# Two transformer layers on one core: a new order of the blocks in each Mamba pair

## The reference

```python
proj = hidden_states @ in_proj_w                 # gate 4096, x 4096, B 128, C 128, dt 64
hbc = silu(causal_conv4(hbc) + conv_b)           # x, B and C
dt = softplus(dt + dt_bias); cum = cumsum(dt * A)            # within a chunk
scores = (C_c @ B_c) * exp(cum_i - cum_j) * dt_c             # i >= j
Y_diag = scores @ x_c
states = (exp(cum_last - cum) * dt_c, B_c, x_c)              # then scanned over the chunks
Y_off  = (C_c, prev_states) * exp(cum)
hidden = (Y_diag + Y_off + D * x) * silu(gate)
hidden = hidden * rsqrt(mean(hidden**2) + EPS) * norm_w
out = hidden @ out_proj_w
```

## Time and profile before

| | |
|---|---|
| runs | 1966.39, 1969.08, 1969.34 us; median 1969.08 |
| profiled execution | 1966.99 us, of which the span 1965.2 |
| TensorE busy | 1911.9 us, 97% of the span |
| VectorE, ScalarE, GpSimd busy | 1532.6, 1310.2, 830.7 us |
| granted TensorE clock, mean | 0.994 |

### The profile page before, as it was taken

The page is one execution under the profiler, slowest core; times in us unless marked ns, Lnnn a source line. Parts: engine busy times, 40 slices in busy tenths (PEclk is TensorE's granted clock), DMA queues, the critical chain, the costliest instruction groups (busy, mean ns, idle before and its releaser), DMA issues.

```text
span 1965.2 us, 43300 instructions
## 1 busy us (share of the span) xinstructions
PE 1911.9 (97%) x12642; PEld 1607.5 (82%) x12642; DVE 1532.6 (78%) x2860; ACT 1310.2 (67%) x2983; POOL 830.7 (42%) x997
## 2 busy tenths in 40 slices
PE   7999999999999999999999999999999999999998
PEld 7888778888888968888878886888888888788886
DVE  6886678888788468888878836888888883688886
ACT  4663389999555148888845514888875551588885
POOL 2210268888200016777710001777770000177776
PEclk9999999999999999999999999999999999999999
DMA  6330356656422114444422211544442221244442
GB/s 231 120 120 1 124 162 207 203 193 208 134 75 85 52 46 156 146 155 148 164 77 84 75 62 35 168 146 157 146 153 86 91 62 49 83 146 156 146 153 78
DMA packets 122051, 239.86 MB, mean 122 GB/s; under 512 B 10832, under 2 KB 48912, under 8 KB 121872
## 3 DMA queue, kind: packets, MB, share of 16 engines
q1 hardware_dynamic: 122000, 239.18, 37.2%
HBM read 198.37 MB, written 37.62 MB: 120 GB/s over the span
## 4 chain that ended last, share of the span: by engine, by line
PE 71%; issue 20%; DVE 5%; ACT 2%; POOL 1%; DMA 0%; POOLq 0%; DVEq 0%; ACTq 0%
PE bank L695 31%; PE bank L965 12%; PE bank L952 6%; PE bank L941 5%; PE bank L932 4%; PE bank L924 3%; PE both L695 2%; PE bank L845 2%; PE bank L802 2%; DVE conv_acc L1428 1%; PE both L802 1%; PE bank L772 1%; PE bank L777 1%; PE bank L854 0%; ACT bank L1166 0%
## 5 line engine op out<-in xcount | busy, mean ns | idle before, releaser
L695 PE MATMUL bank<-xn_r,w_r 128*128 128x512 f32 x2268 | 610.6, 409 | 4.2 <-issue 3.2
L695 PEld LDWEIGHTS bank<-xn_r,w_r 128*128 128x128 f32 x2268 | 413.1, 189 | 104.9 <-issue 27.2
L1428 DVE SCALAR_TENSOR_TENSOR conv_acc<-bank,conv_sb,conv_acc 128x511 f32<-128x511 f32 (+2 forms) x408 | 304.3, 746 | 39.0 <-ACT conv_acc L1161 5.3
L570 POOL TENSOR_TENSOR rstd<-var_eps,minus_half 128x4 f32<-128x4 f32 (+2 forms) x12 | 9.7, 808 | 627.9 <-DVE var_eps L1357 627.9
L965 PE MATMUL bank<-wo_n,place 128*128 128x256 f32 x1024 | 255.1, 392 | 1.6 <-DVE place L1606 1.6
L1344 DVE TENSOR_TENSOR place_r<-bank,place_r 128x512 fp32r<-128x512 f32 (+1 forms) x320 | 186.7, 632 | 76.2 <-ACT place_r L1084 76.2
L1084 ACT ACTIVATE place_r<-bank 128x512 fp32r<-128x512 f32 (+1 forms) x320 | 159.2, 556 | 126.0 <-PE bank L695 98.7
L591 POOL TENSOR_TENSOR shared<-shared,c_t 128x768 f32<-128x768 f32 x128 | 234.4, 1831 | 6.6 <-ACT shared L1262 6.6
L965 PEld LDWEIGHTS bank<-wo_n,place 128*128 128x128 f32 x1024 | 184.0, 189 | 43.2 <-issue 21.2
L613 POOL TENSOR_TENSOR sumsq<-sumsq,place 128x512 f32<-128x512 f32 x127 | 161.9, 1275 | 114.8 <-ACT place L1150 114.8
L695 PE MATMUL bank<-place_r 128*128 128x512 f32 (+3 forms) x960 | 188.9, 337 | 8.4 <-DVE place_r L1344 6.0
(11 more groups left out here) (163 smaller groups left out, 3597.0 us busy)
## 6 DMA issues: line engine op xcount, KB each, us to landing
place_r<-cum_rows SPq DMA_DIRECT2D x128, 512.0 KB, 3.9
w_r<-pair_split SPq DMA_DIRECT2D x96, 512.0 KB, 3.7
w_r<-qkv_split SPq DMA_DIRECT2D x48, 512.0 KB, 4.0
pair_split<-w_r SPq DMA_DIRECT2D x32, 512.0 KB, 4.0
qkv_split<-w_r SPq DMA_DIRECT2D x16, 768.0 KB, 3.9
w_r<-qkv_split SPq DMA_DIRECT2D x48, 256.0 KB, 3.2
wo_n<-out_split SPq DMA_DIRECT2D x96, 128.0 KB, 3.6
raw<-in_w_pair SPq DMA_DIRECT2D x32, 256.0 KB, 3.9
```

The source lines that it names most:

```text
L695: ins = mm(out, lhsT=w(a), rhs=m(b), start=(start and i == 0), stop=(stop and i == 2), **kw)
L1428: stt(out=conv_acc[:, back:W], in0=src[:, 0:W - back], scalar=conv_sb[:, ch, TAPS - 1 - back:TAPS - back], in1=conv_acc[:, back:W], op0=AL ...
```

## The change

TensorE's order in pair n becomes: gate(n+1), x(n+2), transposes(n+1), out(n-1), in(n), off(n), states(n+1). So states are made one pair ahead, states(0) before the first pair, and the off-block follows the in-block of the same pair. All four transposes go into bank 2 (before: two into bank 0 and two into bank 2), and `weighted` is one instruction in place of two. `project_gate` waits no longer for half of `x_dt`. ScalarE, VectorE, GpSimd and SyncE are put in a matching order: GpSimd begins a pair with `carry_states`, then prepares the next (`weigh_c`, then `weigh_x`; before it was `weigh_x` first); ScalarE begins with the copy of the states. In batch 0 the split of the weights runs one pair further ahead.

```diff
 # GpSimd
-                def pair(n, par, ahead, before=2):
-                    if before > 1:
-                        add_squares(b, n - 2)
+                def prepare(n, par):
+                    weigh_c(b, n, par)
                     weigh_x(b, n, par)
+
+                def pair(n, par, ahead, before=1):
+                    carry_states(b, n)
                     if ahead and first(b):
-                        split_low(NH + n + 2, par, 2 * D)
-                    weigh_c(b, n, par)
-                    carry_states(b, n)
+                        split_low(NH + n + 3, 1 - par, 2 * D)
+                    prepare(n + 1, 1 - par)
+                    if before > 0:
+                        add_squares(b, n - 1)
 
                 pool.wait_ge(s_dec_ready, b + 1)
+                if first(b):
+                    split_low(NH + 2, 0, 2 * D)
+                prepare(0, 0)
 # TensorE
             def project_gate(b, n, par):
                 pe.wait_ge(s_gate_ready, b * NPAIR + n + 1)
-                pe.wait_ge(s_xdt_half, b * NPAIR + n + 1)
                 project(bank[0][:], par, 0).then_inc(s_w_used, 1)
...
-                    if before > 0:
-                        turn_x(b, n, par)
-                        off_block(b, n - 1, 1 - par)
-                    if not more and not last:
-                        pe.wait_ge(s_xdt_half, (b + 1) * NPAIR + 1)
+                    if more:
+                        project_gate(b, n + 1, 1 - par)
+                    elif not last:
+                        pe.wait_ge(s_gate_ready, (b + 1) * NPAIR + 1)
                         pe.wait_ge(s_taps_done, (b + 1) * (NPAIR + 2))
                         first_qk(b + 1)
+                    if ahead:
+                        project_x(b, n + 2, par)
                     if more:
-                        project_gate(b, n + 1, 1 - par)
-                    make_states(b, n, par)
-                    if before == 0:
+                        turn_x(b, n + 1, 1 - par)
+                    if before > 0:
+                        project_out(b, n - 1, 1 - par, isinstance(n, int) and n == 1, False)
+                    else:
                         pe.wait_ge(s_res_ready, b + 1)
                     in_block(b, n, par)
-                    if before > 0:
-                        project_out(b, n - 1, 1 - par, isinstance(n, int) and n == 1, False)
-                    if ahead:
-                        project_x(b, n + 2, par)
-
+                    off_block(b, n, par)
+                    if more:
+                        make_states(b, n + 1, 1 - par)
+
+                make_states(b, 0, 0)
                 pair(0, 0, True, True, before=0)
 # ScalarE, inside pair(n): after the copy of the states
                     if more:
-                        mixes(n + 1, 1 - par)
                         act.wait_ge(s_state_ev, N + 2)
                         conv_tanh(K + n + 3, bank[2])
-                        growth(n + 1, 1 - par)
                     if not begin:
                         squares(b, n - 1)
+                    if more:
+                        gate_tanh(b, n + 1, 1 - par)
+                        if deep and first(b):
+                            w_high(NH + n + 3, 1 - par, 2 * D)
+                        growth(n + 1, 1 - par)
+                        if ahead:
+                            pair_conv_start(b, n + 2)
+                        mixes(n + 1, 1 - par)
+                        if ahead:
+                            spans(n + 2, par)
 # VectorE
-                mixed(b, 0, 0)
                 weighted(b, 0, 0)
...
                     if not begin:
-                        weighted(b, n, par)
                         base, gated = tail(n - 1, 1 - par)
                         base()
                         gated()
                     if more:
-                        if not begin:
-                            conv_taps(K + n + 3, ch, bank[1])
-                            dve.wait_ge(s_hid_ready, N + 1)
+                        conv_end(K + n + 3, xs[:, 1 - par, :], bank[2])
+                    mixed(b, n, par)
+                    if more:
                         pair_gate(b, n + 1, 1 - par)
-                        conv_end(K + n + 3, xs[:, 1 - par, :], bank[2])
-                        mixed(b, n + 1, 1 - par)
+                        weighted(b, n + 1, 1 - par)
+                        if ahead:
+                            conv_taps(K + n + 4, n + 2 if isinstance(n, int) else bass.ds(n + 2, 1), bank[1])
```

More of the change, by code:

```diff
@@ L473, in first_sequence @@
                     spread_load(0, n, n)
+                pair_save(0, 0)
+                pair_load(2, 0)
                 for n in range(2):
[L475 to L476 removed]
+                    pair_save(n + 1, 1 - n)
+                    pair_load(n + 3, 1 - n)
                     spread_load(0, n + 2, n)
                     out_load(n, n)
[L479 removed]
+                with sp.Fori(1, NPAIR // 2 - 2) as i:
                     for par in range(2):
[L481 to L482 removed]
+                        pair_save(i * 2 + par + 1, 1 - par)
+                        pair_load(i * 2 + par + 3, 1 - par)
                         spread_load(0, i * 2 + par + 2, par)
@@ L485, in first_sequence @@
                         out_load(i * 2 + par, par)
[L486 to L489, removed]
+                for n in range(NPAIR - 4, NPAIR):
+                    par = n % 2
+                    if n + 1 < NPAIR:
+                        pair_save(n + 1, 1 - par)
+                    if n + 3 < NPAIR:
+                        pair_load(n + 3, 1 - par)
+                    if n + 2 < NPAIR:
+                        spread_load(0, n + 2, par)
+                    out_save(n - 2, par)
+                    out_load(n, par)
                 for par in range(2):
@@ L920, in turn_x @@
                 pe.wait_ge(s_conv_silu, N + b * 2 + 4)
[L921 to L925, removed]
+                for t in range(NT):
+                    ins = pe.transpose(bank[2][:, t * P:(t + 1) * P], xs[:, par, t * P:(t + 1) * P], ident[:])
+                ins.then_inc(s_x_turned, 1)
             def make_states(b, n, par):
@@ L1270, in mixes @@
                     A(both[:], span[par].rearrange("p h w -> p (h w)"), ACT.Exp, scale=-1.0).then_inc(s_mix_exp, 1)
+                if first(b):
+                    w_high(NH + 2, 0, 2 * D)
                 act.wait_ge(s_cum_t_ready, b + 1)
@@ L1278, in sequence, with pair @@
                 growth(0, 0)
-                def pair(n, par, more, ahead, begin=False):
+                def pair(n, par, more, ahead, deep, begin=False):
                     N = b * NPAIR + n
-                    if more and not begin:
-                        pair_conv_start(b, n + 1)
-                    if ahead and first(b):
-                        act.wait_ge(s_w_used, N + 1)
-                        w_high(NH + n + 2, par, 2 * D)
-                    elif not ahead and not last and par == 1:
-                        if first(b):
-                            act.wait_ge(s_gu_saved, 32)
-                        qk_high(b + 1, 0, copied=(b + 1) * 64)
-                    if more:
-                        if not begin:
-                            spans(n + 1, 1 - par)
-                        gate_tanh(b, n + 1, 1 - par)
                     act.wait_ge(s_state_done, N + 2)
@@ L1298, in pair @@
                     if more:
-                        mixes(n + 1, 1 - par)
                         act.wait_ge(s_state_ev, N + 2)
                         conv_tanh(K + n + 3, bank[2])
-                        growth(n + 1, 1 - par)
                     if not begin:
                         squares(b, n - 1)
+                    if more:
[8 more added lines that the diff above has]
+                            spans(n + 2, par)
+                    elif not last:
+                        if first(b):
+                            act.wait_ge(s_gu_saved, 32)
+                        qk_high(b + 1, 0, copied=(b + 1) * 64)
                     if first(b):
                         out_high(n, par)
-                pair(0, 0, True, True, begin=True)
-                pair(1, 1, True, True)
-                with act.Fori(1, NPAIR // 2 - 1) as i:
+                pair(0, 0, True, True, True, begin=True)
+                pair(1, 1, True, True, True)
+                with act.Fori(1, NPAIR // 2 - 2) as i:
                     for par in range(2):
-                        pair(i * 2 + par, par, True, True)
-                pair(NPAIR - 2, 0, True, False)
-                pair(NPAIR - 1, 1, False, False)
+                        pair(i * 2 + par, par, True, True, True)
+                pair(NPAIR - 4, 0, True, True, True)
+                pair(NPAIR - 3, 1, True, True, False)
+                pair(NPAIR - 2, 0, True, False, False)
+                pair(NPAIR - 1, 1, False, False, False)
                 if not last:
@@ L1608, in tail, with pair @@
                     return base, gated
```

(5 more changed lines are left out.)

32 lines of the change are left out of this document (14 added, 18 removed).

## The result

The changed kernel takes 1956.19 us (median of 5 runs, 1953.81 to 1959.05), the kernel before on the same chip 1967.22 us (5 runs, 1965.42 to 1969.34). The ratio is 0.9946, 95% interval 0.9932 to 0.9959: faster by half a per cent. The profiled execution took 1958.19 us, its span 1956.3.

A forecast was written before the change was run, and what follows sets the result against it. TensorE, busy for 97% of the span, was taken to bound the kernel. Terms -29.6 + 14.4 + 6.0 + 1.2 = -8.0 us took the profiled 1966.99 to 1959.0, plus 2.1 to the median: 1961.1 us, range 1945 to 1981.

The forecast's parts named there:

- pairs, batches 1 to 3: TensorE makes one 64-column visit a pair instead of two: 7.81 to 7.47 us a pair, 29.6 us gained.
- pairs, batch 0: ScalarE, with GpSimd's loop much the same, holds batch 0's pair at 7.7 to 7.8 us: 0 gained, bounds -6 and +4.
- starts, with the clock: At each batch's start TensorE waits for `x_w` behind `c_grow`: 14.4 us lost, plus 6.0 us for the half clock after it.
- ends: From gate(31) to the sum of squares: +0.5 us in each of the first three batches, last 0.3 better; 1.2 us lost.
- The step: In the pairs, the off-block's own 64-column visit disappears from TensorE's order, saving 0.34 us a pair, bounds 0 and 0.36.
- The narrow count for VectorE: In the new pair VectorE has 0.1 us of margin up to the next base, and 0.5 more before it delays conv_end.
- Rival B: Another engine, first VectorE, sets the pair: at 7.65 us a pair 1976.8 us, slower; chance 0.17.
- GpSimd makes `c_grow` before `x_w`: At each batch's start `c_grow` waits for growth(0), so `x_w` is late and TensorE stands from 739.5 until 743.2.
- after every idle stretch of 2.85 us or more: Inside the run TensorE's granted clock is 0.50 (1.2 GHz, not 2.4) for a while after such a stretch.
- The forecast of the half clock behind the new stall: A new 3.7 us idle stretch at each start brings the half clock: 1.6 us each, 6 us lost, bounds 0 and 7.

The follow-up runs named there:

- dve_plus_psum: Changed kernel with one added, unused 128x512 multiply a pair on VectorE, second input from PSUM, ahead of the taps: 1957.10 us, ratio 0.9959 to the kernel before.
- first_x: Changed kernel with GpSimd making `x_w` before `c_grow` for pair 0 of each batch only: 1940.61 us, ratio 0.9868 to the kernel before.
- fill: Changed kernel with 16 added 128x128 float32 products on TensorE ahead of each batch's first states: 1950.47 us, ratio 0.9915 to the kernel before.
- dve_plus2: Changed kernel with two added, unused 128x512 multiplies a pair on VectorE, inputs from SBUF, behind the taps: 2099.68 us, ratio 1.0676 to the kernel before.

## Why the prediction was right, point by point

The forecast was 1961.1 us with a sum of -8.0 us against the profiled execution; the profiled times differ by -8.8 us, the spans by -8.9, the medians by -11.0. By its own terms, read between the same marks (last product of the down-projection, gate(2), gate(31), sum of squares) in both traces:

| term | forecast | traces |
|---|---|---|
| pairs, batches 1 to 3 | -29.6 | -28.1 |
| pairs, batch 0 | 0 | -2.9 |
| starts, with the clock | +14.4 + 6.0 | +19.9 |
| ends | +1.2 | +1.3 |
| everything else | 0 | +0.9 |

The mechanisms came as forecast; that the sum came out within 1 us is in part luck, for batch 0's pairs gained 2.9 us more than forecast, batches 1 to 3 gained 1.5 less, and the rest lost 0.9.

*The pairs.* 7.49 us, not 7.47: a visit is worth 0.32 us here. The step holds, and the swap of four products shows that it is the tile. The reading of single gaps was rougher than the sum. I counted the off-block's own visit, 0.17 + 0.17 us; what stands around the one visit left is 0.33 + 0.17 = 0.50, against 0.64 around the two before, and the other 0.18 us of the gain is in the seams between blocks of one tile, where the next loads now start up to 0.07 us before the block in front has ended. A tile change on one side and a seam on the other can't be priced apart from one row.

*The other engines.* The narrow count for VectorE was good: 0.1 + 0.5 us of slack forecast, 0.66 us measured by added work in batches 1 and 2 (0.75 in batch 3). Timeline of the changed kernel, conv_end and its reader:

```profile
867.71 0.69 DVE L1453 SCALAR_TENSOR_TENSOR place<-bank,conv_acc 128x512 f32<-128x512 f32 x1 [0.45 <-ACT bank L1179]
...
868.95 0.60 PE L936 MATMUL bank<-ident,place 128*128 128x128 f32 x4
```

VectorE waits 0.45 us for the tanh, and conv_end is ready 0.55 us before the transposes (0.6 forecast). Rival B did not happen, and dve_plus_psum stands where it would begin.

*Batch 0.* 7.74 us a pair, in the 7.7 to 7.8 that I gave. Against the 7.83 before, that range makes 1 to 4 us gained over 29 pairs; I put nothing for it, and 2.9 us it was: the term with the largest miss. Which engine set it was left open between ScalarE and GpSimd's loop; shortening GpSimd's wait gave next to nothing, relieving ScalarE gave everything down to 7.49.

*The starts.* In batches 1 to 3 the way from the down-projection to gate(2) grew by 5.7, 6.1 and 5.8 us, 0.8 of it for states(1): 4.9 to 5.3, against 3.4 + 1.5 forecast. Batch 0 lost 4.6 us where I had 5.5. So the term came out 0.5 us too large; its 14.4 is 14.2 by its own parts (4 x 3.4 + 0.6). first_x and fill show what is in it: the stall with its cause is the order on GpSimd, the clock 5.7 us (6 forecast).

*The ends.* In the first three batches gate(31) to the sum of squares takes 19.8 to 19.9 us (20.0 forecast); transposes(31) wait 0.55 us for conv_end and out(31) 0.92 us. The last batch takes 13.1 us (13.2 forecast).

"Everything else" is the stages the change does not touch; both traces have half-clock stretches there, and they don't fall alike.

The change thus gave back 21 of its 31 us in short places at the start and the end of each batch. The part of the prediction that could have been turned into a better kernel was "GpSimd makes `c_grow` before `x_w`": swapping those two lines is worth 23 us.

## What to carry to other kernels

When work is moved a step ahead, look at the first turn of the loop by itself: what is ready early inside the loop can be the last thing to be ready in front of it, and each queue's order should follow who needs what first there. Group products by tile shape: each visit to a 64-column tile costs 0.32 to 0.35 us here, as much as three of the pair's four transposes (0.43 us for the four), though TensorE shows no wait. Before giving an engine with time to spare another instruction, look at where its operands lie and at what its neighbour is doing at that moment.

## What the runs showed that I had not expected

VectorE's instructions whose inputs all lie in SBUF waited for GpSimd's. The same 128x512 multiply took 0.68 us with one input in PSUM, 1.16 us (1.69 in batch 0) with both in SBUF, ending each time about 0.55 us after a GpSimd instruction of 1.28 us; a scaling of 128x256 took 1.43 us beside GpSimd's whole addition, and 0.35 where GpSimd's instruction had 0.1 us left. It goes both ways: in dve_plus2 GpSimd's carry, 0.40 us elsewhere, takes 0.83 while the second multiply runs. Timeline of dve_plus2:

```profile
903.88 1.77 DVE L1637 TENSOR_TENSOR spare<-c_t 128x512 f32<-128x512 f32 x2
...
905.08 0.83 POOL L609 TENSOR_TENSOR carry<-state,dec 128x128 f32<-128x128 f32 x1 [0.58 <-ACT state L1093]
```

The Trainium skill says so, page "SBUF — State Buffer", section "Who interferes with whom": a VectorE instruction with both inputs in SBUF contends with GpSimd's reads, and the later one blocks until the first has finished. These rows agree for the multiply. The scaling has one tensor as input (`raw_out`) beside a column of factors, which that sentence does not speak of; the rows show that it waits as well. In this kernel all nine of VectorE's instructions of a pair have an operand in PSUM, so the slack of 0.66 us is only there for work of that kind, or for work that meets an idle GpSimd.

The clock: 3.60 us of idle TensorE brought a stretch at 0.50 in all four batches; in first_x 2.83 us before states(1) of batch 0 did not (granted 1.00 from 263.92 on), and 1.61 us did not in the other three, while the kernel before has 2.85 us of idle with 0.50 behind it. The prediction's "after every idle stretch of 2.85 us or more" holds for the trace before and not for the one after: the same stall in front of line 894, 2.85 us in batch 1 and 2.86 in batch 3, was followed by the full clock once and by the half clock once. Windows of the changed kernel behind the two:

```profile
709.81:712.81 3.00, 3.00 (x22) 2.77 (x23) 2.81 (x5) 0.75 (x2) 0.00 (x0) 1.00 0.19 44
1671.56:1674.56 3.00, 3.00 (x14) 3.00 (x15) 2.03 (x4) 0.76 (x2) 0.00 (x0) 0.50 0.19 44
```

So near 3 us it is not the length of the idle stretch alone, and what else decides stays open. The forecast of the half clock behind the new stall was right for stalls of 3.60 us; these traces would not have borne it out for one of 2.85.
